# A four-layer graph network: the adjacency is stored beside dense layers 2 and 3 in place of 1 and 2

## What is computed

```python
edge_index = jnp.stack([src, dst])
x = _layernorm(x + _L0_gnn_ref(x, ..., edge_index), axis=-1)   # two convolutions, log_softmax
x = _layernorm(x + _L1_gnn_ref(x, edge_index, ...), axis=-1)   # segment_sum(x[src], dst), two-layer MLP
x = _layernorm(x + _L2_gnn_ref(edge_index, edge_type_100, x, ...), axis=-1)   # per edge: ccorr(x[dst], rel[type])
x = _layernorm(x + _L3_gnn_ref(x, ..., src, dst), axis=-1)     # segment_sum(h[src], dst) @ W, batch norm, elu
return x
```

## Time and profile before

| What | us |
|---|---|
| Median of 3 runs (3242.05 to 3258.43) | 3250.92 |
| The profiled execution | 3241.18 |
| Its span (first to last instruction) | 3239.1 |

### The profile page before, as it was taken

The page is one execution under the profiler, slowest core; times in us unless marked ns, Lnnn a source line. Parts: engine busy times, 40 slices in busy tenths (PEclk is TensorE's granted clock), DMA queues, the critical chain, the costliest instruction groups (busy, mean ns, idle before and its releaser), DMA issues.

```text
span 3239.1 us, 43437 instructions
## 1 busy us (share of the span) xinstructions
PE 2018.7 (62%) x12631; PEld 1573.1 (49%) x12632; DVE 1646.2 (51%) x4098; ACT 1322.7 (41%) x3259; POOL 1972.7 (61%) x2030
## 2 busy tenths in 40 slices
PE   0078878467665765555655555566666666666667
PEld 0066544234433665555655555454555555555544
DVE  7989999545653432222222222364445454454453
ACT  4289766000311543333533333253333453333322
POOL 0777777312222777777777777377777777777700
PEclk9555565578786655555555555687777787777778
DMA  1000000084101222222222221252233322333281
GB/s 38 1 2 2 2 2 2 17 156 80 12 5 43 68 60 52 53 53 53 53 53 53 53 53 35 81 127 78 77 78 79 78 78 76 78 79 79 60 184 30
DMA packets 172646, 183.05 MB, mean 57 GB/s; under 512 B 68506, under 2 KB 145414, under 8 KB 171667
## 3 DMA queue, kind: packets, MB, share of 16 engines
q1 hardware_dynamic: 100801, 99.30, 14.1%
q0 software_dynamic: 64960, 78.47, 9.9%
q10 hardware_dynamic: 6656, 2.40, 0.3%
HBM read 153.41 MB, written 26.60 MB: 56 GB/s over the span
## 4 chain that ended last, share of the span: by engine, by line
POOL 43%; issue 18%; DVE 16%; PE 11%; DMA 7%; ACT 3%; DVEq 1%; SPq 0%; PEldq 0%; PEld 0%; ACTq 0%; POOLq 0%
POOL adj_again_middle L1622 43%; DMA sorted_edges<-block_rows,run_rows 4%; DVE adj L688 4%; DVE oh_dst L717 3%; PE psum L1165 3%; DMA adj_again_middle<-gather_table,gidx_s 2%; PE psum L1161 2%; DVE runs L453 1%; ACT sq_src L656 1%; PE psum L1742 1%; PE psum L763 1%; DVE adj_again_middle L1694 1%; DVE rank L462 1%; ACT oh_src L668 1%; DMA l_v<-in_L_gnn_beta 1%
## 5 line engine op out<-in xcount | busy, mean ns | idle before, releaser
L1622 POOL DMA_INDIRECT adj_again_middle<-gather_table,gidx_s x1568 | 1508.3, 962 | 552.5 <-issue 469.9
L1694 DVE TENSOR_TENSOR adj_again_middle<-adj_again_middle,psum 128x256 f32<-128x256 f32 x1176 | 442.1, 417 | 1140.2 <-DMA adj_again_middle<-gather_table,gidx_s 830.1
L1742 PE MATMUL psum<-rel_parts,oh_t 128*128 128x96 bf16 (+1 forms) x4704 | 566.6, 289 | 709.2 <-DVE adj_again_middle L1694 557.7
L1662 ACT ACTIVATE adj_again_middle<-cst,lo_s 128x125 f32<-128x125 f32 x1664 | 527.1, 388 | 1074.6 <-PE psum L1778 1068.7
L1742 PEld LDWEIGHTS psum<-rel_parts,oh_t 128*128 128x128 bf16 x4704 | 415.8, 127 | 830.2 <-issue 587.9
L1778 PE MATMUL psum<-adj_again_middle,oh_s 128*125 x3328 | 741.1, 382 | 20.9 <-issue 16.1
L1778 PEld LDWEIGHTS psum<-adj_again_middle,oh_s 128*125 128x125 f32 x3328 | 663.2, 288 | 46.5 <-issue 40.0
L296 POOL DMA_INDIRECT sorted_edges<-rec,row_i x392 | 393.1, 1003 | 214.6 <-issue 128.5
L763 PE MATMUL psum<-oh_dst,oh_src 128*125 128x300 bf16 (+2 forms) x784 | 338.1, 522 | 73.3 <-DVE oh_dst L717 54.7
L1666 ACT ACTIVATE oh_s<-adj_again_middle,cst 128x500 f32<-128x500 f32 x416 | 296.1, 712 | 13.6
L1434 POOL DMA_INDIRECT sorted_edges<-block_rows,run_rows x64 | 69.5, 1086 | 299.8 <-ACT block_rows L1423 227.4
(11 more groups left out here) (408 smaller groups left out, 1411.6 us busy)
## 6 DMA issues: line engine op xcount, KB each, us to landing
tb<-sorted_types SPq DMA_DIRECT2D x392, 128.0 KB, 3.2
adj_again_middle<-gather_table,gidx_s POOLq DMA_INDIRECT x1568, 2.5
adj_saved<-adj SPq DMA_DIRECT2D x6, 2734.4 KB
adj_again_middle<-adj_saved SPq DMA_DIRECT2D x3, 2734.4 KB
sorted_edges<-rec,row_i POOLq DMA_INDIRECT x392
adj_again_last<-adj_saved SPq DMA_DIRECT2D x2, 2734.4 KB
adj_again_first<-adj_saved SPq DMA_DIRECT2D x1, 2734.4 KB
adj_saved<-adj SPq DMA_DIRECT2D x6, 317.4 KB
```

Of the source, the lines that this page charges most:

```text
L1622: nc.gpsimd.indirect_dma_start(gx[g % DEEP][:, k, :], None, table_d[d], bass.IndirectOffsetOnAxis(ap=gidx_s[:, t:t + 1], axis=0),).then_in ...
L1662: sq = nc.scalar.activation(sq_s[:, k, :], iota[:, 0:LO], ACT.Square, bias=lo_s[:, t:t + 1], scale=-1.0)
L1694: mul = v.tensor_tensor(part_prod[:, u * SUB:(u + 1) * SUB, s, :].rearrange("p g (a f) -> p g a f", a=2), rows[:, :, s * d // 2:(s + 1) * ...
L1742: mm = nc.tensor.matmul(ps_rel[:, k * RS:k * RS + W], oh_t[g % (AHEAD + 1)][:, (u * SUB + k) * P:(u * SUB + k + 1) * P], rel_parts[:, s, : ...
```

## The change

The first dense layer gets no `save`. The second stores chunks 0 to 3 and the third chunks 4 to 6.

```diff
             dense(counted_adj, parts12, parts3, ident_b, left, room, True, False, [w[:, 0, :]], first_post,
-                                    save=lambda sp: keep_adjacency(sp, range(0, 4)), steps=steps_of(0))
+                                    steps=steps_of(0))
...
             dense(counted_adj, parts12, parts3, ident_b, left, room, True, False, [w[:, 1, :]], second_post, second_act,
-                  save=lambda sp: keep_adjacency(sp, range(4, CHUNKS)), steps=steps_of(1))
+                  save=lambda sp: keep_adjacency(sp, range(0, 4)), steps=steps_of(1))
...
             dense(counted_adj, parts12, parts3, ident_b, left, room, True, True, [w_sum[:], w_own[:], b1[:], w2[:]], hidden_post,
-                  steps=steps_of(2))
+                  save=lambda sp: keep_adjacency(sp, range(4, CHUNKS)), steps=steps_of(2))
```

## The result

The changed kernel takes 3232.95 us (median of 8 runs, 3226.28 to 3236.86), the kernel before in the same comparison 3250.53 (8 runs, 3242.05 to 3258.43). The ratio is 0.9944 with a 95% interval of 0.9931 to 0.9958: 17.6 us faster, or 0.56%. The forecast was 3231 us, 19.5 us faster. Two later comparisons gave 0.9943 (0.9920 to 0.9965) and 0.9937 (0.9920 to 0.9953).

What follows compares the result with a forecast made beforehand. It took landings of the second-half sort's scatters, slowed by stores, as the dense layers' largest share (31.1%). Layers 1, 2 and 3 gave -35 + 2.5 + 13 = -19.5 us, from median 3250.9 to 3231; range 3216 to 3250.

Steps and rivals of the forecast that it cites:

- Layer 1, 77 us forecast: First dense layer without stores: 77 us instead of 112.3, a gain of 35 us, 29 with the slower ends.
- GpSimd keeps up and hands no backlog to layer 2: Layer 1's sort: 25 scatters take 74 us within the layer's 77, so none is left to land in layer 2.
- Layer 2, 119.7 us (bounds 115 to 125): Second dense layer storing four chunks instead of three: 119.7 us against 117.2, cost 2.5 us, bounds -2 to +8.
- the marks of 128 and 108: Signs of a wrong forecast: layer 2 taking over 128 us, or layer 3 over 108.
- Layer 3, 102 us (bounds 97 to 108): Third dense layer storing three chunks: waits at sort steps 10 and 11, cost 13 us over 88.9, bounds 8 to 19.
- Nothing is lost again: Layer 3 behind step 11: landings are short from the fifth scatter on, so no further time is lost.
- What hides the rest: Loads between layers meet an empty queue; the last store ends about 41 us into layer 3, so L1585 adds no wait.
- The sum, -19.5 us: Whole kernel: -35 + 2.5 + 13 = -19.5 us, with ends of -31 to -2.
- The stall is conserved: Rival, chance 0.20: each stored chunk slows equally many scatters anywhere, layers 2 and 3 give back layer 1's gain; 3251 us.
- VectorE's port: Rival, chance 0.05: VectorE's bf16 sort work, not the stores, holds up GpSimd's descriptors; landings stay slow in layer 1; 3251 us.
- Layer 3 without slack: Rival, chance 0.06: each slow landing beyond the lead costs layer 3 8.5 us; three past the stores give +6, four +15.

Runs made afterwards that it cites:

- after_again: The changed kernel, unedited, profiled a second time: median 3221.49 us, ratio 0.9943 to the kernel before.
- before_again: The kernel before, unedited, profiled a second time: median 3243.34 us, ratio 1.0012 to the kernel before.
- stores_late: `save` left out of all three layers, all seven chunks stored after layer 3: median 3296.51 us, ratio 1.0178 to the kernel before.
- after_third: The changed kernel, unedited, profiled a third time: median 3226.11 us, ratio 0.9937 to the kernel before.

## Why the prediction was right, and where it was off

**Layer 1, 77 us forecast:** 77.2 to 78.4 measured in every run without stores beside it. Right, and so is the gain of 35 within its bounds (29 to 35): 112.3 or 110.5 less 78.4 is 32 to 34. The layer took up to 1.4 us more than forecast, and the second profile of before started 1.8 us lower.

**"GpSimd keeps up and hands no backlog to layer 2":** wrong. The step priced a scatter at 2.13 us and 0.8 behind it, 2.93 in all. In layer 1 of the changed kernel the 25 scatters went out from 661.67 to 742.93, one every 3.39 us, and the last of them fell into layer 2's stores (742.93, 9.77 us). The copy of that last step had been ready since 730.78, so GpSimd was 12 us behind. So layer 2's first scatter went out at +8.1 to +8.9 us where layer 1's had gone out at +4.5. The price was small all the same: the layer's sixth scatter goes out when the stores end, whether or not one of layer 1 stands ahead of its five slow ones, and with stores at 200 GB/s layer 2 took 117.7.

**Layer 2, 119.7 us (bounds 115 to 125):** 117.7, 120.9 and 128.1. The working holds: the sixth landing was taken at +66.9 and came at +66.0, +69.0 and +73.9, and from there to the layer's end 52.8 us were taken and 51.8, 51.9 and 54.3 measured. The bounds were too narrow: they allowed for half a landing of shift, and not for stores that are a tenth slower through the whole layer. The first profile, with 128.1 here and 108.7 in layer 3, even lies just past the marks of 128 and 108 that were named as signs of a wrong forecast; the other two lie below them.

**Layer 3, 102 us (bounds 97 to 108):** 102.7, 106.5 and 108.7. The place was right, steps 10 and 11 (937.25 and 944.13 above, behind waits of 12.11 and 2.46 us). The wait at step 11 was in the first profile only; in the other two TensorE waits at step 10 alone (11.39 and 12.39 us). The third landing came at +42 to +43 us where +39.8 was taken over from layer 1: the third scatter took 13.6 to 14.5 us in place of 10.66, and it met the last chunk's short rows, which layer 1 had not stored. That this is why was not tested. The fourth landing came at +46 (after_again) to +50. "Nothing is lost again" behind step 11 left out a term: the forecast took half clock for one product only, but TensorE stayed at the granted clock 0.50 for 3 to 13 us behind step 10, and that stretch made most of the way from 102.7 to 106.5 (2.8 of 3.8 us) and, with the second wait, to 108.7.

**What hides the rest:** right. No wait at L1585, and the loads between the layers met no stores: the gap between layers 2 and 3 is 21.3 us in both kernels.

**The sum, -19.5 us:** -17.6 by the runs. In the layers the profiles show -3 for the first pair, and -14 and -21 against before_again; the forecast stands for stores at 200 GB/s. In the means of the profiles the three terms are -33.0, +3.9 and +16.7 us where -35, +2.5 and +13 were forecast, -12.5 in all: each missed to the same side. The runs lie nearer the forecast (-17.6, and by the ratios of the later comparisons some -18 and -20): the profiled executions of before lay 4 us under their medians in the mean, those of the changed kernel 2 above. So the sum is right within what these profiles can tell, but that it came out within 2 us is in part luck, as one execution's layers differ by 16 us from another's.

**The rivals.** *The stall is conserved* falls: the ratio lies below 1 with its whole interval in three comparisons, the layers took 299 to 315 us against 318 to 320, and it is the lead that decides, by the runs with more buffers. It came closest in the first profile, where stores at 179 GB/s left 3 us of the gain. *VectorE's port* falls as the cause of the slow landings (stores_late, and layer 1 of the changed kernel). *Layer 3 without slack* did not turn the sign: its slow landings ended with the stores.

## What to carry to other kernels

Here a bulk transfer beside a chain of small transfers cost what the chain's lead didn't cover, not what the bulk transfer took: count how many steps the consumers may run ahead, how long that lasts at the layer's own pace, and put the bulk where steps are sparse. Against the same layer without stores, four chunks cost layer 1 33 to 35 us and layer 2, with fewer steps in a chunk, 17 to 28. Better still, lengthen the lead: four more buffers of 48 bytes per partition brought the changed kernel another 25 to 30 us, more than the move's 17.6, and with fourteen more the place of the stores no longer showed in the time. And before a difference between two profiles is explained, take a second profile of each, since here one execution of the same kernel had 16 us more in this stretch than another.

## What the runs showed of the hardware

A scatter of 120 rows of 48 bytes lands in 2.1 us on an idle queue and in 8.7 to 14.5 us while stores from SyncE's queue fill the 16 DMA engines (profiles with six buffers). It was not quicker when those stores moved 75 GB/s in rows of 250 bytes in place of some 200 in rows of 1000: scatters that met the short rows took 10.67 us (811.38 in the earlier trace rows) to 14.54 (912.11 in after_again), others 8.66 (799.89 in after_again) to 14.40 (890.79 in after_third). How the engines share their time between the two was not tried.

When a long wait of TensorE ended, its granted clock was 0.50 in layer 3 of all three profiles of the changed kernel, and stayed so for 3 to 13 us: a wait cost more than its own length, 1.6 us more in the second profile and 4.4 in the third.

GpSimd's own instruction for a scatter takes 0.98 us, but of the 18 in the first profile of the changed kernel that started while VectorE's L1391 was running, 13 took 1.4 to 2.2; of the 46 that started at another time, one took over 1.3. Timeline of both engines in layer 1, where nothing is stored:

```profile
697.01 1.15 DVE L1391 TENSOR_TENSOR block_ones<-iota_b,block_t 98x960 bf16<-98x960 bf16 x1
...
697.36 1.66 POOL L1434 DMA_INDIRECT sorted_edges<-block_rows,run_rows  x1 [1.95 <-ACT block_rows L1423]
```

So 13 of 18 such meetings cost 0.5 to 1.2 us. In layer 1 they come to 4.8 us over 25 scatters, 0.2 of the 0.46 us by which GpSimd's pace of 3.39 us lies above 2.93.

The Trainium skill, "SBUF — State Buffer", says in its box on the "DVE blocks DMA" trap that GpSimd is locked out of a shared port pair and cannot write descriptors while VectorE runs an operation in a two-port mode. L1391 is a TENSOR_TENSOR, and of this operation the Trainium skill says on the same page, under "Who interferes with whom", that it has no two-port mode but contends with GpSimd's reads when both its inputs are in SBUF. So the rows are not the trap as the box has it. That they are the second case was not tested.
